# First expert tile outside the loops, other PSUM banks, packed tile borders and earlier gathers in a graph and mixture-of-experts layer

## The reference

```python
flat = layernorm(layernorm(x)) * ln_scale + ln_bias
h_shared = swiglu(flat @ shared_in_w.T)
out_shared = h_shared @ shared_out_w.T + shared_out_b
g_idx = argmax(flat @ group_gate_w.T + group_bias)         # 2 groups of 4 experts
e_probs = softmax(e_logits of that group)
topv, topi = top_k(e_probs, 2); topv = topv / (topv.sum(-1) + 1e-8)
h_expert = swiglu(flat @ expert_in_w.T)                    # one hidden row for all experts
for e in range(8):
    routed += comb[:, e:e+1] * (h_expert @ expert_out_weight[e].T)
x = x + out_shared + routed
```

## Time and profile before

| | us |
|---|---|
| median of 3 runs | 771.73 |
| lowest and highest run | 771.67 and 780.08 |
| the profiled execution | 776.86 |
| its span, from the first to the last instruction | 774.9 |

### The profile page before, as it was taken

How to read it: one execution, slowest core, us unless ns; L and a number is a source line. 1 busy time by engine, 2 the same in 40 slices (tenths; PEclk the granted TensorE clock), 3 DMA queues, 4 the chain that set the end, 5 groups by cost and what they waited for, 6 DMA issues and landing times.

```text
span 774.9 us, 12228 instructions
## 1 busy us (share of the span) xinstructions
PE 734.6 (95%) x4377; PEld 450.8 (58%) x4377; DVE 410.4 (53%) x802; ACT 262.8 (34%) x387; POOL 169.5 (22%) x166
## 2 busy tenths in 40 slices
PE   5989999999799999989999999999799999999998
PEld 5655677776366655656665654445644545555554
DVE  5977977894357767687435432222155524421154
ACT  4842222221373222325534223333354624422000
POOL 2330000000007000002212234444512122211362
PEclk9998999999799999999999999999989999999999
DMA  9200002000012133001143311111268766433674
GB/s 245 85 1 1 1 1 110 1 1 14 0 63 76 56 109 109 1 0 42 49 141 120 94 40 56 55 51 34 81 221 319 248 230 231 123 122 130 184 206 137
DMA packets 24274, 73.39 MB, mean 95 GB/s; under 512 B 7043, under 2 KB 7389, under 8 KB 20130
## 3 DMA queue, kind: packets, MB, share of 16 engines
q1 hardware_dynamic: 8607, 39.74, 15.3%
q0 software_dynamic: 10624, 24.99, 11.3%
q10 hardware_dynamic: 4994, 8.01, 2.8%
HBM read 57.38 MB, written 15.31 MB: 94 GB/s over the span
## 4 chain that ended last, share of the span: by engine, by line
PE 77%; DVE 8%; ACT 7%; DMA 3%; issue 2%; ACTq 1%; DVEq 0%; SPq 0%
PE banks L1272 58%; PE banks L1314 6%; PE banks L1302 6%; DMA y_rows<-xT 3%; PE banks L1615 2%; ACT W L411 1%; DVE st L742 1%; PE banks L1486 1%; PE banks L1295 1%; DMA x<-in_x 1%; PE banks L1329 1%; PE banks L1495 1%; ACT xn L564 1%; ACT xn L561 1%; DVE xn L1092 1%
## 5 line engine op out<-in xcount | busy, mean ns | idle before, releaser
L1272 PE MATMUL banks<-W,xT 128*125 128x512 f16 (+1 forms) x1392 | 319.7, 384 | 10.9 <-ACT xT L686 4.9
L1272 PEld LDWEIGHTS banks<-W,xT 128*125 128x125 f16 (+1 forms) x1392 | 166.0, 122 | 140.9 <-issue 20.0
L1272 PE MATMUL banks<-xT,W 128*128 128x500 f16 (+1 forms) x720 | 132.1, 346 | 1.8 <-DVE xn L1224 1.4
L1272 PEld LDWEIGHTS banks<-xT,W 128*128 128x128 f16 x720 | 70.9, 99 | 61.1 <-issue 5.2
L719 DVE SCALAR_TENSOR_TENSOR W<-stg,W 128x2048 f16<-128x2048 f32 x30 | 68.5, 2304 | 42.6 <-ACT W L411 42.6
L1272 PE MATMUL banks<-W,big 128*125 128x512 f16 x360 | 81.5, 380 | 0.0
L1242 DVE CAST xT<-banks 128x1024 f32 x23 | 28.1, 1223 | 74.3 <-PE banks L1615 74.3
L1272 PEld LDWEIGHTS banks<-W,big 128*125 128x125 f16 x360 | 48.3, 136 | 29.2 <-issue 2.3
L353 POOL DMA_INDIRECT xn<-h_rows,tokidx x28 | 35.0, 1251 | 127.6 <-PE banks L1615 122.0
L342 POOL TENSOR_TENSOR big<-xn,big 125x512 f16<-125x512 f32 x20 | 23.5, 1173 | 174.8 <-ACT big L603 174.8
L411 ACT ACTIVATE W<-stg 128x2048 f16<-128x2048 f32 x30 | 56.4, 1903 | 0.0
(11 more groups left out here) (287 smaller groups left out, 852.7 us busy)
## 6 DMA issues: line engine op xcount, KB each, us to landing
stg<-in_units SPq DMA_DIRECT2D x30, 1024.0 KB, 5.2
y_rows<-xT ACTq DMA_DIRECT2D x29, 256.0 KB, 4.9
h_rows<-big POOLq DMA_DIRECT2D x10, 500.0 KB, 3.6
out_x<-x SPq DMA_DIRECT2D x10, 224.0 KB
stg<-in_wqkT SPq DMA_DIRECT2D x2, 1024.0 KB, 11.4
x<-in_x SPq DMA_DIRECT2D x2, 896.0 KB
x<-in_x SPq DMA_DIRECT2D x1, 448.0 KB
xn<-h_rows,tokidx POOLq DMA_INDIRECT x28, 5.1
```

The source lines that it names most:

```text
L1272: ins = te.matmul(dst, lhs(sl, c), rhs(sr, c), start=(first and c == 0 and k == 0), stop=(last and c == n - 1 and k == 2))
```

## The change

- `turned` (where tiles are turned) moves from banks 0 to 3 to banks 4 to 7, and the expert product from bank 4 to bank 0. `sobank`, the order of banks in the shared output product, is rotated to fit.
- TensorE turns tile 0 before it loads the borders and without the wait for `h_f`. Tile 1 is turned and tile 0 multiplied in straight code ahead of the loops; the matmul of the bias row is gone. The loops begin at tile 1. The counts that the engines wait for (`me_mm`, `y_cp`, `y_st`) are one lower, the shift of the slots by 128 is gone. Expert 0 gets at least two tiles.
- ScalarE and VectorE copy tiles 0 and 1 out before they convert the two units of expert 2.
- VectorE packs the eight last tile numbers as two integers of four digits in base `PACK` = 28. Each engine makes two loads in place of eight (`borders`). ScalarE and VectorE do them in step 21 of the shared product.
- GpSimd scatters twice in each of the steps 0 to 9, reads the table in step 11 and gathers tiles 0 and 1 in step 12.
- `NT` grows from 27 to 28 and `NG` from 28 to 29, so that there is one more gather, and with total = 23 there are six dummy stores in place of five.

The core of the diff:

```diff
-NT = (TOPK * NODES - EXP) // ST + EXP
+NT = (TOPK * NODES - EXP) // ST + EXP + 1
 NG = NT + 1
+PACK = NT
...
-        turned = [PS[:, 2 * z:2 * z + 2, :].rearrange("p b (j n) -> p (b j) n", n=ST) for z in range(2)]
-
-        sobank = [ps[i] for i in (5, 6, 7, 0, 1, 2, 3, 4)]
+        turned = [PS[:, 4 + 2 * z:6 + 2 * z, :].rearrange("p b (j n) -> p (b j) n", n=ST) for z in range(2)]
+
+        sobank = [ps[i] for i in (1, 2, 3, 4, 5, 6, 7, 0)]
...
+        def borders(eng):
+
+            ends = []
+            for z in range(2):
+                four = eng.value_load(etab[0:1, z:z + 1], min_val=0, max_val=PACK ** 4 - 1)
+                for k in range(4):
+                    e = 4 * z + k
+                    ends.append(eng.snap((four // PACK ** k) % PACK + 1, min_val=e + 1, max_val=NT - EXP + e + 1))
+            return ends
...
-                    if n < TOPK * TILES:
-                        k, t = n % TOPK, n // TOPK
+                    for m in (2 * n, 2 * n + 1) if n < TILES else ():
+                        k, t = m % TOPK, m // TOPK
                         g.indirect_dma_start(tok_of, bass.IndirectOffsetOnAxis(ap=sloti[:, 1, k, t:t + 1], axis=0),
                                              tokid[:, t:t + 1], None).then_inc(S["tok_put"], 16)
-                    if n == TOPK * TILES:
+                    if n == TILES + 1:
                         pool.wait_ge(S["tok_put"], 16 * TOPK * TILES)
                         g.dma_start(tokidx[:, :], tok_of.rearrange("(p i) o -> p (i o)", p=128)).then_inc(S["tok_ld"], 16)
-                    if n == TOPK * TILES + 1:
+                    if n == TILES + 2:
...
-                    act.wait_ge(S["me_mm"], ends[what[1]] + 1)
+                    act.wait_ge(S["me_mm"], ends[what[1]])
...
+                    if n == 21:
+                        act.wait_ge(S["etab_rdy"], 1)
+                        ends = borders(act)
+                        total = ends[EXP - 1]
...
-                act.wait_ge(S["me_mm"], i + 1)
-                act.wait_ge(S["y_st"], 16 * i + 16)
-                s.activation(yb, ps[4][:, :], ACT.Copy).then_inc(S["y_cp"], 1)
-                act.wait_ge(S["y_cp"], i + 1)
-                act.dma_start(y_rows[bass.ds(i * ST, ST), :], yb).then_inc(S["y_st"], 16)
+                act.wait_ge(S["me_mm"], i)
+                act.wait_ge(S["y_st"], 16 * i)
+                s.activation(yb, ps[0][:, :], ACT.Copy).then_inc(S["y_cp"], 1)
+                act.wait_ge(S["y_cp"], i)
+                act.dma_start(y_rows[bass.ds((i - 1) * ST, ST), :], yb).then_inc(S["y_st"], 16)
...
             act.wait_ge(S["turned"], 1)
             s.activation(hgT[:, 0, 0], turned[0], ACT.Copy).then_inc(S["hg_h"], 1)
+            act.wait_ge(S["turned"], 2)
+            s.activation(hgT[:, 1, 0], turned[0], ACT.Copy).then_inc(S["hg_h"], 1)
             unit(U_EXP + 4)
             unit(U_EXP + 5)
             for e in range(EXP):
-                with act.Fori(0 if e == 0 else starts[e - 1], ends[e]) as i:
+                with act.Fori(1 if e == 0 else ends[e - 1], ends[e]) as i:
...
-            with act.Fori(total + 1, NT + 2) as i:
+            with act.Fori(total, NT + 1) as i:
...
-                link(v.tensor_scalar(nt8[:, 0, :], nt8[:, 0, :], 1.0, None, ALU.max))
+                link(v.tensor_scalar(nt8[:, 0, 0:1], nt8[:, 0, 0:1], 2.0, None, ALU.max))
+                link(v.tensor_scalar(nt8[:, 0, 1:EXP], nt8[:, 0, 1:EXP], 1.0, None, ALU.max))
...
+                ends8 = seen[0:1, TILES, :]
+                link(v.scalar_tensor_tensor(out=ends8, in0=nt8[0:1, 1, :], scalar=-1.0, in1=nt8[0:1, 0, :], op0=ALU.add, op1=ALU.add))
+                pairs = ends8.rearrange("p (z a b) -> p z a b", z=2, a=2)
+                link(v.scalar_tensor_tensor(out=etabf[:, 0:4].rearrange("p (z a) -> p z a", z=2), in0=pairs[:, :, :, 1], scalar=float(PACK), in1=pairs[:, :, :, 0],
+                                            op0=ALU.mult, op1=ALU.add))
+                quads = etabf[:, 0:4].rearrange("p (z a) -> p z a", z=2)
+                v.scalar_tensor_tensor(out=etab[:, :], in0=quads[:, :, 1], scalar=float(PACK * PACK), in1=quads[:, :, 0],
+                                       op0=ALU.mult, op1=ALU.add).then_inc(S["etab_rdy"], 1)
...
             hgT2 = xflat[:, 0:2 * ROWW]
-            pe.wait_ge(S["h_f"], 3 * J)
             pe.wait_ge(S["cntT_ev"], 3)
             pe.wait_ge(S["g_rdy"], 1)
             turn(lambda o: hg2[:, o:o + 128])
-
-            te.matmul(ps[4][:, :], ones16[0:2, :], rows16[:, :], start=True, stop=True).then_inc(S["me_mm"], 1)
+            pe.wait_ge(S["etab_rdy"], 1)
+            ends = borders(pe)
+            total = ends[EXP - 1]
+
+            def expert(e, cur):
+                split3(ps[0][:, :], lambda s, c: hgT2[:, cur(s * HID + c * 128)], unitv(U_EXP + 2 * e), J, True, True).then_inc(S["me_mm"], 1)
+
+            pe.wait_ge(S["hg_h"], 1)
+            pe.wait_ge(S["hg_l"], 1)
+            pe.wait_ge(S["g_rdy"], 2)
+            turn(lambda o: hg2[:, ROWW + o:ROWW + o + 128])
+            pe.wait_ge(S["w_rdy"], U_EXP + 2)
+            pe.wait_ge(S["h_f"], 3 * J)
+            expert(0, lambda o: slice(o, o + 128))
             for e in range(EXP):
                 pe.wait_ge(S["w_rdy"], U_EXP + 2 * e + 2)
-                with pe.Fori(0 if e == 0 else starts[e - 1], ends[e]) as i:
+                with pe.Fori(1 if e == 0 else ends[e - 1], ends[e]) as i:
                     pe.wait_ge(S["hg_h"], i + 1)
                     pe.wait_ge(S["hg_l"], i + 1)
                     pe.wait_ge(S["g_rdy"], i + 2)
                     nx = pe.snap(((i + 1) % 2) * ROWW)
                     turn(lambda o: hg2[:, bass.ds(nx + o, 128)])
-                    pe.wait_ge(S["y_cp"], i + 1)
+                    pe.wait_ge(S["y_cp"], i)
                     cur = pe.snap((i % 2) * ROWW)
-                    split3(ps[4][:, :], lambda s, c: hgT2[:, bass.ds(cur + (s * HID + c * 128), 128)], unitv(U_EXP + 2 * e), J,
-                           True, True).then_inc(S["me_mm"], 1)
+                    expert(e, lambda o: bass.ds(cur + o, 128))
```

More of the change, by code:

```diff
@@ L176, in build @@
         tokidx = sb("tokidx", [128, NG], I32)
-        etab = sb("etab", [1, EXP + 1], I32)
+        etab = sb("etab", [1, 2], I32)
+        etabf = sb("etabf", [1, 6])
         cnt9 = sb("cnt9", [P, TILES, 18])
@@ L204, in build @@
         h_rows = nc.dram_tensor("h_rows", (NODES, ROWW), F16).ap()
-        y_rows = nc.dram_tensor("y_rows", ((NT + 2) * ST, DIM), F32).ap()
+        y_rows = nc.dram_tensor("y_rows", ((NT + 1) * ST, DIM), F32).ap()
         tok_of = nc.dram_tensor("tok_of", (NG * ST, 1), I32).ap()
@@ L388, in _ @@
             pool.nop().then_inc(S["g_rdy"], 1)
-            pool.wait_ge(S["y_st"], 16 * (NT + 3))
+            pool.wait_ge(S["y_st"], 16 * (NT + 2))
             for t in range(TILES):
@@ L672, in _ @@
                         unit(U_EXP + n // 4 - 1)
-            act.wait_ge(S["etab_rdy"], 1)
-            starts = [act.value_load(etab[0:1, e:e + 1], min_val=e, max_val=NT - EXP + e) for e in range(1, EXP + 1)]
-            ends, total = starts, starts[EXP - 1]
+                    if n == 21:
+                        act.wait_ge(S["etab_rdy"], 1)
+                        ends = borders(act)
+                        total = ends[EXP - 1]
             def high(i):
@@ L1199, in route @@
                 link(v.tensor_reduce(slotf[:, 0], pick[:, :, :, :], AX.X, ALU.add))
-                v.tensor_scalar(sloti[:, 0], slotf[:, 0], float(ST), None, ALU.add).then_inc(S["slots_rdy"], 1)
+                v.tensor_copy(sloti[:, 0], slotf[:, 0]).then_inc(S["slots_rdy"], 1)
                 link(v.tensor_scalar(slotf[:, 1], slotf[:, 0], -(ST - 1) / 2, 1.0 / ST, ALU.add, ALU.mult))
@@ L1229, in _ @@
                         unit(U_EXP + n // 4 - 1)
-            dve.wait_ge(S["etab_rdy"], 1)
-            starts = [dve.value_load(etab[0:1, e:e + 1], min_val=e, max_val=NT - EXP + e) for e in range(1, EXP + 1)]
-            ends, total = starts, starts[EXP - 1]
+                    if n == 21:
+                        dve.wait_ge(S["etab_rdy"], 1)
+                        ends = borders(dve)
+                        total = ends[EXP - 1]
             dve.wait_ge(S["turned"], 1)
             v.tensor_copy(hgT[:, 0, 1], turned[1]).then_inc(S["hg_l"], 1)
+            dve.wait_ge(S["turned"], 2)
+            v.tensor_copy(hgT[:, 1, 1], turned[1]).then_inc(S["hg_l"], 1)
             unit(U_EXP + 4)
@@ L1239, in _ @@
             for e in range(EXP):
-                with dve.Fori(0 if e == 0 else starts[e - 1], ends[e]) as i:
+                with dve.Fori(1 if e == 0 else ends[e - 1], ends[e]) as i:
                     dve.wait_ge(S["turned"], i + 2)
@@ L1246, in _ @@
             with dve.Fori(total, NG) as i:
-                dve.wait_ge(S["me_mm"], total + 1)
+                dve.wait_ge(S["me_mm"], total)
                 dve.wait_ge(S["g_rdy"], i + 2)
@@ L1616, in turn @@
```

(6 more changed lines are left out.)

2 lines of the change are left out of this document (removed).

## The result

| | before | changed |
|---|---|---|
| median of 20 runs each | 773.31 us | 768.69 us |
| lowest to highest | 770.67 to 780.08 | 765.86 to 771.41 |
| profiled execution (its span) | 776.86 (774.9) | 768.86 (767.0) |

The ratio is 0.9929, with a 95% interval of 0.9907 to 0.9951: 5.5 us less, between 3.8 and 7.2 (the two medians are 4.6 us apart). Measured again later (after_again), the changed kernel had 0.9956 (0.9931 to 0.9981), 3.4 us less. The forecast was 769.4 us, which is close to the 768.69 measured. But the forecast gain was 2.3 us, from a median of 771.73 over three runs, and here the kernel before has a median of 773.31.

What follows compares the result with a forecast made beforehand. TensorE was taken as the bound, busy 734.6 of 774.9 us. The terms summed to -2.3 us, from tile 2 starting sooner, the others taken as nothing: 771.73 to 769.4 us, range 765.8 to 773.3.

Steps and rivals of the forecast that it cites:

- the mechanism at the borders: Between shared product and tile 2: first tiles start sooner, then late weights hold tile 2; gain 2.3 us.
- Turn 0 at the signal: Behind the shared product: TensorE's first turn waits only for GpSimd's signal at 556.8, starting at 557.0, 1.5 us earlier.
- the earlier gathers bring nothing: Shared product: issuing gathers nine steps earlier gains nothing, since GpSimd's signal still stands behind step 23.
- Turn 1 and tile 0: Behind the first turn: second turn at about 560.1 us, tile 0's product between 561.3 and 562.6 against 565.93.
- Unit 7 sets tile 2: Before tile 2: ScalarE waits for weights landing at 575.1 us; tile 2 starts at 577.8 against 580.08, gain 2.3.
- The low clock costs nothing more: Up to tile 2: half clock adds no time, since the tiles before wait for the late weights anyway.
- The other four stalls stay: Expert loops: TensorE's four waits for ScalarE's result copies, 4.9 us in all, remain, moments shifting -1.5 to +1.5 us.
- The end: Kernel's end: one more gather and store delay result gathers 1.3 to 3.1 us, inside 3.29 us idle; nothing.
- Routing, scatters, ScalarE's loads in step 21: Up to the shared product's end: extra work fits idle time; nothing, bounds 1 us for routing, 2.4 for unpacking divisions.

Runs made afterwards that it cites:

- after_again: The changed kernel with no edit, timed again with a second trace; ratio 0.9956 against the kernel before.
- gathers_late: Changed kernel with one scatter per step, the table read in step 20 and the gathers of tiles 0 and 1 in step 21; ratio 0.9947.
- early_loads: Kernel before with ScalarE's and VectorE's eight border loads made in steps 19 and 21, and TensorE's behind turn 0; ratio 1.0005.
- late_shift: Changed kernel with the late weight units one expert later, none after expert 0's loop; ratio 0.9887 against the kernel before.
- unit_between: Changed kernel with unit 4 converted between the copies of tiles 0 and 1 on ScalarE and VectorE; ratio 0.9892 against the kernel before.
- before_again: Kernel before with no edit, one execution for a second trace; shared product ended at 549.99 us against 555.24.
- before_spread: Kernel before with 60 do-nothing instructions in TensorE's list, three behind each half node tile of the expert hidden product; ratio 0.9970.
- one_less: Changed kernel with NT 27 and NG 28, packing base still 28, so one gather and one dummy store less; ratio 0.9948.
- after_padded: Changed kernel with 64 do-nothing semaphore instructions ahead of TensorE's first matmul; ratio 1.0031 against the kernel before.
- after_spread: Changed kernel with 60 do-nothing instructions in TensorE's list, three behind each half node tile of the expert hidden product; ratio 0.9990.

## Why the prediction was right, point by point

The forecast time fits, and so does the mechanism at the borders. The gain does not fit well: 2.3 us was forecast, and 4.6 to 5.5 us were measured, 3.4 the second time.

- **Turn 0 at the signal.** Forecast 1.76 us behind the shared product (557.0), measured 1.51 in every trace of the changed kernel. Right. That the earlier gathers bring nothing held within 0.2 us (gathers_late). early_loads shows the condition: where the gathers start 1.6 us ahead of the end, turn 0 waits for their landing.
- **Turn 1 and tile 0.** Forecast tile 0 at 6.1 to 7.4 us behind the end, measured 5.59: turn 1 began right behind VectorE's copy, 3.93 us behind the end, where I had 4.9. GpSimd's gather for tile 2 did not delay it. I had also laid 1.46 us on turn 0 from a row at a falling clock; it took 1.05.
- **Unit 7 sets tile 2.** Forecast: lands 19.9 us behind the end, tile 2 at 22.6, gain 2.3 us. Measured: landed at 571.26, 19.8; tile 2 at 22.40, gain 2.44. late_shift and unit_between show the cause. The bounds of this term were kept.
- **"The low clock costs nothing more."** This step failed. I had asked only whether half clock ahead of the stop could hide in it. The stop itself, 3.8 us, lowers the clock behind it: +1.7 us or more on tile 2, in the six traces with this border code and the units in this place (stops of 3.8 to 4.6 us). With stops of 1.49, 0.85 and 0 us at tile 2 its matmuls take 5.35 us. This is no rule for shorter stops: around turn 0 the changed kernel stands for 1.51 and 1.36 us, and a spell of 3.4 us at half clock follows, in turn 1 and tile 0.
- **"The other four stalls stay."** Wrong: I gave their moments -1.5 to +1.5 us, and they are worth -3.0. They are three, not four, 3.6 us together: the fourth wait of the earlier trace rows is the 1.33 us ahead of tile 0, which the change removes. And six pairs of units are loaded in the loops, not seven. I had read the stalls as stores against weights and gathers. The fetch queue stands in the page too (31 and 18 packets), and I left it out because its bytes are few.
- **The end.** Forecast start of the first gather 1.3 to 3.1 us later, measured 3.0 (14.92 against 11.89); cover 3.29, measured 1.33 left. Right, with little to spare: in three of the experiments it was used up.
- **Routing, scatters, ScalarE's loads in step 21:** no new wait of TensorE in the trace. Right, and the bounds of 1 to 2.4 us for them were not needed.

So in the two traces the part behind the shared product is some 4 us shorter: -2.4 us up to tile 2, +1.7 for the clock, -0.3 in the tiles and -3.0 for the stalls that go with where the code lies. The other 3.8 us between the two traces lie ahead of the change, and before_again shows that much without an edit. Two terms of opposite sign were missing, and the median of the kernel before turned out 1.6 us higher. That the total came close to 769.4 all the same is luck.

Like against like, the change alone is worth about 1 us or less. With no stall over 1 us behind stores the loops take 156.24 us (before_spread) against 155.20 to 155.95 (changed, after_again, one_less), and with two such stalls 159.25 to 159.76 against 158.66 (after_padded).

## What to carry to other kernels

A wait that is removed early in a pipeline runs into the next transfer: work out when each buffer is refilled in the new order, and put work that waits for a transfer behind the copy that the matmuls wait for. A stop can cost twice, by itself and by the clock behind it: here the stops of 3.8 to 4.6 us cost another 1.7 to 2.4. Before a change of 0.5% is credited to its idea, add some do-nothing instructions to both kernels and see whether the gain moves: here 60 of them took 3.0 us out of one kernel's loops, more than the change itself is worth.

## What the runs showed of the hardware that I had not expected

- A store of 256 KB in flight with weights takes about 7.1 us from issue to landing when a 16 KB instruction fetch falls into it, and about 5.5 without one, in the loops behind tile 2. TensorE then stands for 1.4 to 1.8 us. Three more such fetches made no stall (changed kernel at 578.6 us, after_spread at 574.5 and 642.4), and the store of tile 0 can take 7.1 us with no fetch in its flight (after_again, beside units 6 and 7).
- 64 do-nothing semaphore instructions in a row on TensorE's queue take 9.7 us from the first start to the last (0.8 to 10.5 us), 0.15 us each, though each row reads 51 ns.
- The same kernel reached the same matmul at 549.99 and at 555.24 us. The spells at half clock ahead of it, 3.4 against 20.4 us together, are the visible difference.
